# Local attention's output product moved behind its loop, an output copy put between exponentials, and the first image loaded by ACT's queue

## The chip, the cores and the metric

The kernel runs on one core of a Trainium2 chip. The metric is the device time of one execution in microseconds (us). Engines are called as in the profile: PE (TensorE, with its weight loads as PEld), DVE (VectorE), ACT (ScalarE), POOL (GpSimd), SP (SyncE, which here only issues DMAs; its queue is SPq).

## The reference

Two layers of a vision tower work on four images x of 64 channels x 128 steps x 64 variables. Cut to what matters:

```python
h = tok(x, W)                       # patches, rfft, projection: 1024 tokens x 64 for each image
h = h + local_attn(layernorm(h))    # the part that the change touches
h = h + moe_top2(layernorm(h))
h = h + full_attn_batchnorm(layernorm(h))
h = h + routed_moe(layernorm(h))
# local_attn: 16 query heads of 64, one key/value head, RoPE, RMS norm,
#   a token sees itself and the 128 before it; softmax; then
out = einsum('bqgts,bqgsd->bqgtd', attn, v).reshape(B, T, 16 * 64)
return out @ wo.T                   # 1024 tokens x 1024 -> 1024 x 64
```

## The kernel before, in words

The program is a row of stages, each a block with an instruction list for each engine and a barrier of all engines at its end that clears the semaphores. `setup` runs once; then `tokens`, `project`, `windowed`, `experts` and `full` run for each of the four images (a hardware loop); `batchnorm` and `routed` end it. The order inside a stage is written out by hand, engine by engine, with semaphore waits; no planner is involved.

**setup** (L286). SP issues 35 DMAs one after the other: two for the token weights (semaphore `tok_loaded`), 32 for all other constants, and last, through `load_x`, the 4 MB of image 0 into `xb`. It then waits until all but the first two have landed and raises `x_loaded`. DVE waits for that (L331) and then prepares the constants (`moe_w2`, the split bias, masks, `wqk`, `bvrep`), 5.7 us of work. Beside the loads PE makes 128 small products of the token weights (L360); after DVE's `h_ready` it makes two small ones (L364, L366), and after DVE has copied the token weights (`weff`) the first image's token products (L388: 8 pairs of matmuls with a 64-column weight and 512 moving columns, one to the upper and one to the lower 64 rows of a PSUM bank). ACT copies their result to `tokensT`.

**windowed** (L569). Local attention in 32 chunks of 32 tokens. A chunk passes through: scores on PE (L603 mask, L607 products) into banks 0-1 or 2-3; row maximum on DVE (L669) and the bias made of it (L672, `bias_ready`); four exponentials on ACT (L723, each with a sum); reciprocal on DVE (L688); scaling on POOL (L700, L702, `scaled`); transposes on PE (L627, L628, `turned` into banks 4-5); copy to `pT` on DVE (L682); value products on PE (L644, L641, `pv_done`) into banks 6-7; copy to `oT` (a view of `big2`) on ACT (L711, `oT_ready`). PE's list in step n is scores(n), turn(n-3), values(n-4). ACT's list in step n is the copy of chunk n-4, then the four exponentials of chunk n. scores(n) waits until the exponentials of chunk n-2 are done, since it writes their bank.

The output product with `wo` is made for each 128-token tile i in `out_product(i)` (L613): 8 matmuls with a 128-column piece of `oT` as the weight and 64 moving columns of `wo`. It stands inside `turn(c)` for c = 7, 11, ..., 31, ahead of that chunk's transposes, and DVE adds its result to `h` (L663) ahead of its `pT` copy. In steps 10, 14, ..., 30 six of them stand in the full loop; the seventh (c = 31) stands in the last steps, when scores are over; the eighth comes behind the loop. Then follow the layer norm on DVE, the transposes of `turn_normed` (L271) and the copies to `xT`.

**Other uses of the same helpers.** `turn_halves` (L392) makes four transposes of `tokensT` into bank 3; `tokens` calls it. SP loads the next image in `windowed`, at its start.

Of the kernel before, what the change touches and what calls it, by code (L numbers as in the profile page):

```python
# [25 lines left out]
P = 128  # L26
# [52 lines left out]
def program(nc, inp, out, sent_rows, answered_rows):  # L79
    with ExitStack() as ctx:  # L80
# [13 lines left out]
        big1 = sb("big1", [P, PAIRS, SEQ])  # L94
        big2 = sb("big2", [P, PAIRS, SEQ])
        aside = ("tok_w", "moe_w2")
        sbuf = {k: sb("s_" + k, *shapes[k]) for k in loaded if k not in aside}
# [94 lines left out]
        mean_row, var_row = sb("mean_row", [P, D]), sb("var_row", [P, D])  # L192
        first_sem = sem("const_loaded")
        sems = {n: sem(n) for n in [
# [6 lines left out]
        S = sems  # L201
        clear = range(first_sem.num, S["last"].num + 1)

        def stage(build):

            with nc.Block() as block:
                build(block)
            nc.all_engine_barrier(sems_to_clear=clear)  # L208

# [76 lines left out]
        def setup(block):  # L286
            @block.sync
            def _(sp):
                n = 0
                for k in ("tok_w", "dft"):  # L290
                    sp.dma_start(sbuf[k] if k in aside else sbuf[k][:], inp[k]).then_inc(S["tok_loaded"], 16)
                for k in loaded:
                    if k in ("tok_w", "dft"):
                        continue
                    sp.dma_start(sbuf[k] if k in aside else sbuf[k][:], inp[k]).then_inc(first_sem, 16)
                    n += 1
                for half in range(2):
                    r = slice(D * half, D * half + D)
                    for dst, src in ((row_of_t_rows, "row_of_t"), (window_mask_rows, "window_mask")):
                        sp.dma_start(dst[D * half:D * half + CHUNK], inp[src]).then_inc(first_sem, 16)  # L300
                        n += 1
                    for dst, src in ((qn, "q_norm"), (kn, "k_norm"), (bq, "bq1"), (bk, "bk1")):
                        sp.dma_start(dst[r, :], inp[src]).then_inc(first_sem, 16)
                        n += 1
                sp.dma_start(bvcol[:], inp["bv1"]).then_inc(first_sem, 16)
                n += 1
                for dst, src in ((blrow, "bl1"), (gammarow, "gamma"), (betarow, "beta"), (gate_b, "gate_b"),
                                 (moe_b2_rows, "moe_b2")):
                    sp.dma_start(dst[:] if dst is not moe_b2_rows else dst, inp[src].to_broadcast([P, inp[src].shape[1]])).then_inc(first_sem, 16)
                    n += 1  # L310
                load_x(sp, 0, first_sem)
                n += 1
                sp.wait_ge(first_sem, 16 * n)
                sp.sem_inc(S["x_loaded"], 1)

            @block.vector
            def _(v):
# [11 lines left out]
                ch.step(v.memset(moe_w2[:], 0.0))  # L329
                v.wait_ge(S["x_loaded"], 1)  # L330
                for r in range(2):  # L331
# [21 lines left out]
            @block.tensor  # L353
            def _(pe):
                pe.wait_ge(S["tok_loaded"], 32)
                w = sbuf["tok_w"]
                for o in range(D):
                    for j in range(2):

                        ins = nc.tensor.matmul(bank[0][D * j:D * j + D, o * STRIDE:(o + 1) * STRIDE], w[:, o, :],  # L360
                                               sbuf["dft"][:, j * STRIDE:(j + 1) * STRIDE], start=True, stop=True)
                ins.then_inc(S["tok_done"], 1)
                pe.wait_ge(S["h_ready"], 1)
                nc.tensor.matmul(bank[1][:, 0:D], bvrep[:], sbuf["wl1"][:], start=True, stop=True)  # L364
                for r in range(2):
                    ins = nc.tensor.matmul(bank[1][half_rows(r), D:2 * D], sbuf["wvT1"][:], sbuf["wl1"][:], start=True,  # L366
                                           stop=True)
                ins.then_inc(S["proj_done"], 1)
                pe.wait_ge(S["xn_ready"], 1)
                for r in range(STRIDE):  # L370
                    ins = token_products(r)
                ins.then_inc(S["prod_done"], 1)

            @block.scalar
            def _(a):
                a.wait_ge(S["prod_done"], 1)
                nc.scalar.activation(tokensT, bank[5][:], ACT.Copy)
# [48 lines left out]
        def project(block):  # L426
            @block.tensor
            def _(pe):
# [24 lines left out]
                def q_sums(hh):  # L453
# [6 lines left out]
                    for w in range(2):  # L460
# [4 lines left out]
                        ins.then_inc(S["ssq_done"], 1)  # L465

                for s in range(Q_SUMS[1] + 1):
                    if s < UNITS:
# [52 lines left out]
            def _(v):  # L521
                ch = Chain(v, S["dve_chain"])

                def q_sums(hh):

                    for w in range(2):
# [5 lines left out]
                                                None, ALU.add))  # L532

                for s in range(UNITS):
                    u, c = divmod(s, 2)
# [33 lines left out]
        def windowed(block, b):  # L569
# [11 lines left out]

            def added(c):
                return c % 4 == 3 and c >= 7

            def wo_at(i):
                return bank[5][:, HALF - D * (1 + i % 2):HALF - D * (i % 2)]

            @block.tensor
            def _(pe):
# [22 lines left out]

                def out_product(i):  # L613
                    pe.wait_ge(S["oT_ready"], NQ * (i + 1))
                    for p in range(PAIRS):
                        ins = nc.tensor.matmul(wo_at(i), oT[:, p, P * i:P * i + P], sbuf["wo0"][:, p, :], start=(p == 0),  # L616
                                               stop=(p == PAIRS - 1), skip_group_check=True)
                    return ins

                def turn(c):  # L620
                    pe.wait_ge(S["scaled"], c + 1)
                    if c >= 1:
                        pe.wait_ge(S["pT_ready"], c)
                    if added(c):
                        out_product((c - 7) // 4)
                    for q in range(NQ):
                        nc.tensor.transpose(bank[4][:, P * q:P * q + P], probs[:, c % 3, q, 0:P], ident[:])  # L627
                    nc.tensor.transpose(bank[5][:, 0:P], own[:, c % 2, :], ident[:]).then_inc(S["transposed"], 1)  # L628
# [19 lines left out]
                for n in range(CHUNKS + 4):  # L648
# [4 lines left out]
                    if n >= 4:  # L653
                        values(n - 4)
                out_product(TILES - 1).then_inc(S["wo_done"], 1)
                turn_normed(pe, 1)

            @block.vector
            def _(v):
                ch = Chain(v, S["dve_chain"])  # L660

                def add_out(i):
                    return v.tensor_tensor(h[:, i, :], h[:, i, :], wo_at(i), ALU.add)  # L663

                for n in range(CHUNKS + 3):
# [10 lines left out]
                    if c >= 0:  # L676
                        v.wait_ge(S["transposed"], c + 1)
                        if c >= 2:
                            v.wait_ge(S["pv_done"], c - 1)
                        if added(c):  # L680
                            add_out((c - 7) // 4)
                        v.tensor_copy(pT[:, c % 2, :],  # L682
# [6 lines left out]
                v.wait_ge(S["wo_done"], 1)  # L689
                ch.step(add_out(TILES - 1))  # L690
                layernorm(v, ch, h[:], xn_in_order, tmp, moe, st, TILES)
# [13 lines left out]
            @block.scalar  # L705
            def _(a):
                for n in range(CHUNKS + 4):
                    c = n - 4
                    if c >= 0:
                        a.wait_ge(S["pv_done"], c + 1)  # L710
                        nc.scalar.activation(  # L711
                            oT[:, :, CHUNK * c:CHUNK * (c + 1)].rearrange("p (h a) t -> p h a t", h=2),
                            ps[:, 6:8, 0:P].rearrange("p h (a t) -> p h a t", t=CHUNK),
                            ACT.Copy).then_inc(S["oT_ready"], 1)
                    c = n
                    if c < CHUNKS:
                        a.wait_ge(S["bias_ready"], c + 1)
                        if c >= 3:
                            a.wait_ge(S["transposed"], c - 2)
                        for e in range(2):  # L720
                            for hh in range(2):
                                q = 2 * e + hh
                                nc.scalar.activation(probs[:, c % 3, q, :],  # L723
                                                     bank[2 * (c % 2) + e][:, SPAN * hh:SPAN * hh + SPAN], ACT.Exp,
                                                     bias=small[:, c % 4, 1, q:q + 1], scale=rq[:, c, e, hh:hh + 1],
                                                     accum_out=small[:, c % 4, 2, q:q + 1]).then_inc(S["exp_done"], 1)
                turned_scalar(a, 1)
# [508 lines left out]
        with nc.Fori(0, IMAGES) as b:  # L1236
# [4 lines left out]
            stage(lambda block: full(block, b))  # L1241
        stage(batchnorm)
        stage(routed)
# [84 lines left out]
```

## Time and profile before

| | us |
|---|---|
| three timed runs | 1224.52, 1228.95, 1229.07 (median 1228.95) |
| the profiled execution's own time | 1223.5 |
| its span, first to last instruction | 1221.4 |
| setup, to the first image's copy by ACT | 0 to 51.6 |
| windowed of the first image, PE's first to last matmul | 109.0 to 216.5 |
| granted clock, mean | 0.839 |

The span is what the rows below are read from; about 2 us lie around it. Four windowed stages of some 107 us are a third of the time. A granted clock of 1.00 is 2.4 GHz, 0.50 is 1.2 GHz; a value between is a slice in which it changed. In the time before the first sustained work of PE the record shows 1.00 whatever the matmuls' durations are.

### The profile page before, as it was taken

Reading aid. Unit: us, or ns where it says so; the run is one execution under the profiler, and the core shown is the slowest. Engines: PE = TensorE matmul, PEld = TensorE weight load, DVE = VectorE, ACT = ScalarE, POOL = GpSimd, SP = SyncE. Lnnn points to the kernel's source line nnn. Section 1 sums busy time; section 2 is a strip of 40 time slices with the busy share of each in tenths; the row PEclk is TensorE's granted clock in tenths of the full one; section 3 lists DMA queues with packets and bytes.
Section 4 is the critical chain, followed back from the end, with each engine's and each line's share of the span. In section 5 each row is a group of like instructions: output and inputs, shape, how many; then the busy total and the mean of one; then the engine's idle time right before and its main releaser. Section 6 shows DMA issues by size and latency. Waiting matters only on the chain. (4 is left out here: it accounts for less than half of the span.)

```text
span 1221.4 us, 19579 instructions
## 1 busy us (share of the span) xinstructions
PE 848.1 (69%) x7278; PEld 579.6 (47%) x7278; DVE 689.3 (56%) x1470; ACT 441.1 (36%) x1363; POOL 338.9 (28%) x372
## 2 busy tenths in 40 slices
PE   4376997775869978858699787585997777120820
PEld 4133775554337755543377555433776455120620
DVE  0376665754766657537666574476665753830335
ACT  0023874232248742322487423224874232000200
POOL 0044543000445420004454200044543000027055
PEclk9987999897879998878799888778998889655865
DMA  7024000000330000003300000034000003000212
GB/s 239 35 54 151 2 2 2 1 1 3 62 143 2 2 2 1 1 3 61 144 2 2 2 1 1 2 56 149 2 2 2 1 1 97 8 8 26 72 40 45
DMA packets 51473, 43.52 MB, mean 36 GB/s; under 512 B 46484, under 2 KB 47956, under 8 KB 50452
## 3 DMA queue, kind: packets, MB, share of 16 engines
q1 hardware_dynamic: 49318, 40.03, 11.2%
q0 software_dynamic: 2048, 2.10, 0.6%
q8 instruction: 63, 1.03, 0.4%
q14 instruction: 44, 0.36, 0.1%
HBM read 29.33 MB, written 4.72 MB: 28 GB/s over the span
## 5 line engine op out<-in xcount | busy, mean ns | idle before, releaser
L723 ACT ACTIVATE work<-ps,small,rq 128x160 f32<-128x160 f32 x512 | 240.4, 487 | 50.7 <-DVE small L672 50.0
L700 POOL TENSOR_TENSOR work<-work,small 128x512 f32<-128x512 f32 x128 | 133.0, 1039 | 215.9 <-DVE small L688 215.9
L669 DVE TENSOR_REDUCE ps<-ps 128x4 f32<-128x640 f32 x128 | 106.5, 832 | 87.9 <-PE ps L607 87.9
L260 PE MATMUL ps<-xT,s_proj_w 64*128 64x512 f32 x384 | 120.6, 762 | 26.8 <-PEq L208 14.5
L682 DVE COPY pT<-ps 128x640 f32<-128x640 f32 x128 | 105.2, 822 | 5.0 <-PE ps L628 5.0
L723 ACT ACTIVATION_READ_ACCUMULATOR work<-ps,small,rq 128x1 f32 x512 | 106.9, 209 | 0.0
L607 PE MATMUL ps<-kT,big 64*128 64x160 f32 x1024 | 106.6, 331 | 0.0
L566 POOL TENSOR_TENSOR big<-xb 128x1024 f32<-128x1024 f32 x32 | 75.7, 2376 | 54.4 <-DVE xb L539 54.4
L260 PEld LDWEIGHTS ps<-xT,s_proj_w 64*128 64x128 f32 x384 | 45.5, 241 | 87.5 <-issue 63.9
L644 PE MATMUL ps<-pT,vwin 128*64 128x128 f32 x1024 | 84.2, 285 | 2.4 <-ACT big L711 2.4
L627 PE MATMUL ps<-s_ident,work 128*128 128x128 f32 x512 | 83.6, 286 | 1.4 <-DVE pT L682 1.2
L607 PEld LDWEIGHTS ps<-kT,big 64*128 64x128 f32 x1024 | 83.5, 207 | 0.4
L711 ACT ACTIVATE big<-ps 128x256 f32<-128x256 f32 x128 | 49.1, 384 | 89.7 <-PE ps L641 89.7
L616 PE MATMUL ps<-s_wo,big 128*128 128x64 f32 x512 | 65.7, 283 | 3.2 <-ACT big L711 2.0
L490 ACT ACTIVATE big<-ps 128x1024 f32<-128x1024 f32 x32 | 32.7, 1023 | 95.6 <-DVE xb L539 95.6
L627 PEld LDWEIGHTS ps<-s_ident,work 128*128 128x128 f32 x512 | 56.2, 146 | 19.8 <-issue 18.8
L616 PEld LDWEIGHTS ps<-s_wo,big 128*128 128x128 f32 x512 | 61.2, 196 | 9.2 <-issue 4.1
L559 POOL MEMSET vwin<- 128x256 f32 x4 | 1.2, 311 | 230.9 <-POOLq L208 230.9
L644 PEld LDWEIGHTS ps<-pT,vwin 128*64 128x64 f32 x1024 | 53.5, 136 | 24.1 <-issue 20.8
L1210 POOL DMA_INDIRECT sent_rows<-big,xb x32 | 30.9, 964 | 114.9 <-DVEq L1162 105.5
L884 PE MATMUL ps<-big 128*128 128x64 f32 x512 | 60.5, 273 | 0.0
L884 PEld LDWEIGHTS ps<-big 128*128 128x128 f32 x512 | 59.8, 193 | 0.0
(236 smaller groups left out, 1411.9 us busy)
## 6 DMA issues: line engine op xcount, KB each, us to landing
xb<-in_x SPq DMA_DIRECT2D x5, 4096.0 KB, 12.7
vrem<-xb SPq DMA_DIRECT2D x64, 64.0 KB, 2.1
s_proj_w<-in_proj_w SPq DMA_DIRECT2D x1, 1536.0 KB, 6.4
sent_rows<-zeros SPq DMA_DIRECT2D x8, 160.0 KB, 3.4
big<-sent_rows SPq DMA_DIRECT2D x5, 256.0 KB, 4.0
answered_rows<-big SPq DMA_DIRECT2D x8, 160.0 KB, 1.8
xb<-in_ffn_w SPq DMA_DIRECT2D x1, 1028.0 KB, 5.7
out<-vrem SPq DMA_DIRECT2D x8, 128.0 KB, 2.1
```

The source lines that it names most:

```text
L260: ins = nc.tensor.matmul(bank[banks + w][:], proj_w[half_rows(w), cols], xT[half_rows(w), :], start=True, stop=True)
L566: g.tensor_tensor(dst, first, second, ALU.add).then_inc(S["rot_done"], 1)
L607: ins = nc.tensor.matmul(tiles[e][:, hh, :], qT[half_rows(e), c, 4 * hh:4 * hh + 4, :].rearrange("p a t -> p (a t)"), kT[half_rows(e), CHU ...
L616: ins = nc.tensor.matmul(wo_at(i), oT[:, p, P * i:P * i + P], sbuf["wo0"][:, p, :], start=(p == 0), stop=(p == PAIRS - 1), skip_group_chec ...
L627: nc.tensor.transpose(bank[4][:, P * q:P * q + P], probs[:, c % 3, q, 0:P], ident[:])
L644: nc.tensor.matmul(o, vwin[:, c, :], pT[:, c % 2, P * q:P * q + P], start=True, stop=True, skip_group_check=True)
L669: ch.step(v.tensor_reduce(row_max(c), ps[:, s_banks(c), 0:2 * SPAN].rearrange("p e (h k) -> p e h k", h=2), X, ALU.max))
L682: v.tensor_copy(pT[:, c % 2, :], ps[:, 4:6, :].rearrange("p a n -> p (a n)")[:, 0:(NQ + 1) * P]).then_inc(S["pT_ready"], 1)
L700: g.tensor_tensor(probs[:, c % 3, :, 0:P], probs[:, c % 3, :, 0:P], bc(small[:, c % 4, 3, :], P), ALU.mult)
L711: nc.scalar.activation(oT[:, :, CHUNK * c:CHUNK * (c + 1)].rearrange("p (h a) t -> p h a t", h=2), ps[:, 6:8, 0:P].rearrange("p h (a t) -> ...
L723: nc.scalar.activation(probs[:, c % 3, q, :], bank[2 * (c % 2) + e][:, SPAN * hh:SPAN * hh + SPAN], ACT.Exp, bias=small[:, c % 4, 1, q:q + ...
L884: ins = nc.tensor.matmul(bank[6 + i % 2][:, 0:D], pT1[:, i % 2, P * k:P * k + P], v1[:, k, :], start=(k == 0), stop=(k == 7))
```

## The change

In `windowed`, `out_product` and its additions leave the loop. Behind it PE waits for all 32 chunks of `oT` and makes 16 products with `wo` as the 64-column weight and 512 tokens as moving columns; ACT copies the bank to `tokensT`, PE transposes it back (`turn_halves`), and DVE adds all 1024 tokens to `h` in one instruction. ACT's copy of chunk c-4 moves from ahead of the four exponentials of chunk c to between the second and the third. In `setup`, ACT issues the first image's load; SP issues first the constants that `setup` needs (`w_loaded`), then the others (`later_sem`, for which PE and DVE wait at the start of `project`), and only behind all of them waits for the first group and raises `set_ready`.

```diff
+        early = ("ident", "wvT1", "wl1", "moe_w2")
...
+        late = [k for k in loaded if k not in early and k not in ("tok_w", "dft")]
+        LATER = 16 * (len(late) + 5)
...
         def setup(block):
...
+                n = 0
+                for k in early:
+                    sp.dma_start(sbuf[k] if k in aside else sbuf[k][:], inp[k]).then_inc(S["w_loaded"], 16)
+                    n += 1
+                sp.dma_start(bvcol[:], inp["bv1"]).then_inc(S["w_loaded"], 16)
+                n += 1
+                for dst, src in ((moe_b2_rows, "moe_b2"), (blrow[:], "bl1")):
+                    sp.dma_start(dst, inp[src].to_broadcast([P, inp[src].shape[1]])).then_inc(S["w_loaded"], 16)
...
+                for k in late:
+                    sp.dma_start(sbuf[k][:], inp[k]).then_inc(later_sem, 16)
+                for half in range(2):
+                    sp.dma_start(bk[D * half:D * half + D, :], inp["bk1"]).then_inc(later_sem, 16)
+                for dst, src in ((gammarow, "gamma"), (betarow, "beta"), (gate_b, "gate_b")):
+                    sp.dma_start(dst[:], inp[src].to_broadcast([P, inp[src].shape[1]])).then_inc(later_sem, 16)
+                sp.wait_ge(S["w_loaded"], 16 * n)
+                sp.sem_inc(S["set_ready"], 1)
...
-                v.wait_ge(S["x_loaded"], 1)
+                v.wait_ge(S["set_ready"], 1)
...
                 pe.wait_ge(S["xn_ready"], 1)
+                pe.wait_ge(S["x_loaded"], 16)
...
+                load_x(nc.scalar, 0, S["x_loaded"])
                 a.wait_ge(S["prod_done"], 1)
...
+                pe.wait_ge(later_sem, LATER)
...
+                v.wait_ge(later_sem, LATER)
...
-                    if added(c):
-                        out_product((c - 7) // 4)
...
-                out_product(TILES - 1).then_inc(S["wo_done"], 1)
+                pe.wait_ge(S["oT_ready"], CHUNKS)
+                for p in range(PAIRS):
+                    for w in range(2):
+
+                        ins = nc.tensor.matmul(bank[0][D * w:D * w + D, :], sbuf["wo0"][:, p, :],
+                                               oT[:, p, w * HALF:(w + 1) * HALF], start=(p == 0), stop=(p == PAIRS - 1))
+                ins.then_inc(S["proj_done"], 1)
+                pe.wait_ge(S["v_act"], 1)
+                turn_halves(S["wo_done"])
                 turn_normed(pe, 1)
...
-                        if added(c):
-                            add_out((c - 7) // 4)
...
-                ch.step(add_out(TILES - 1))
+                by_half = h[:].rearrange("p (w j) d -> p j w d", w=2)
+                ch.step(v.tensor_tensor(by_half, by_half, bank[3][:].rearrange("p (j w d) -> p j w d", w=2, d=D),
+                                        ALU.add))
...
+                def outputs(c):
+                    a.wait_ge(S["pv_done"], c + 1)
+                    nc.scalar.activation(oT[:, :, CHUNK * c:CHUNK * (c + 1)].rearrange("p (h a) t -> p h a t", h=2),
+                                         ps[:, 6:8, 0:P].rearrange("p h (a t) -> p h a t", t=CHUNK),
+                                         ACT.Copy).then_inc(S["oT_ready"], 1)
+
+                for c in range(CHUNKS):
+                    a.wait_ge(S["bias_ready"], c + 1)
+                    if c >= 3:
+                        a.wait_ge(S["transposed"], c - 2)
+                    for q in range(NQ):
+                        if q == 2 and c >= 4:
+                            outputs(c - 4)
+                        e, hh = divmod(q, 2)
+                        nc.scalar.activation(probs[:, c % 3, q, :],
+                                             bank[2 * (c % 2) + e][:, SPAN * hh:SPAN * hh + SPAN], ACT.Exp,
+                                             bias=small[:, c % 4, 1, q:q + 1], scale=rq[:, c, e, hh:hh + 1],
+                                             accum_out=small[:, c % 4, 2, q:q + 1]).then_inc(S["exp_done"], 1)
+                for c in range(CHUNKS - 4, CHUNKS):
+                    outputs(c)
+                a.wait_ge(S["proj_done"], 1)
+                nc.scalar.activation(tokensT, bank[0][:], ACT.Copy).then_inc(S["v_act"], 1)
                 turned_scalar(a, 1)
```

## Rows read from the trace of the kernel before

**Rows 1.** The page: busy time of each engine (share of the span) and instructions.

```profile
PE 848.1 (69%) x7278; PEld 579.6 (47%) x7278; DVE 689.3 (56%) x1470; ACT 441.1 (36%) x1363; POOL 338.9 (28%) x372
```

**Rows 2.** Windows in the loop: bounds, length, busy by engine, clock, DMA share, GB/s.

```profile
128.00:133.00 5.00, 5.00 (x71) 3.55 (x66) 3.77 (x9) 4.52 (x19) 2.79 (x4) 1.00 0.00 0
```

**Rows 3.** Timeline, PE, image 1: start, duration, line, output<-input, count, idle before.

```profile
130.50 0.23 PE L603 MATMUL ps<-window_mask,row_of_t 64*128 64x128 bf16 x2
131.95 0.66 PE L644 MATMUL ps<-pT,vwin 128*64 128x128 f32 x8
132.54 0.45 PE L641 MATMUL ps<-pT,vrem 32*64 32x128 f32 x8
132.93 0.10 PEld L603 LDWEIGHTS ps<-window_mask,row_of_t 64*128 64x128 bf16 x2 [0.18 <-ACT work L723]
...
137.13 0.10 PEld L603 LDWEIGHTS ps<-window_mask,row_of_t 64*128 64x128 bf16 x2 [0.17 <-issue]
```

**Rows 4.** Timeline of ACT and DVE beside it.

```profile
130.63 0.38 ACT L711 ACTIVATE big<-ps 128x256 f32<-128x256 f32 x1 [0.19 <-PE ps L641]
130.91 0.48 ACT L723 ACTIVATE work<-ps,small,rq 128x160 f32<-128x160 f32 x1
132.24 0.16 DVE L672 SCALAR_TENSOR_TENSOR small<-ps,rq 128x4 f32<-128x4 f32 x1
132.66 0.21 ACT L723 ACTIVATION_READ_ACCUMULATOR work<-ps,small,rq 128x1 f32 x1
```

**Rows 5.** Timeline of the end of the loop and of the tail, image 1.

```profile
201.22 2.00 PE L616 MATMUL ps<-s_wo,big 128*128 128x64 f32 x16 [0.29 <-POOL pTr_own L702]
203.05 0.61 PE L627 MATMUL ps<-s_ident,work 128*128 128x128 f32 x4
...
206.43 0.38 ACT L711 ACTIVATE big<-ps 128x256 f32<-128x256 f32 x1 [1.25 <-PE ps L641]
206.87 2.00 PE L616 MATMUL ps<-s_wo,big 128*128 128x64 f32 x16 [0.50 <-ACT big L711]
208.90 0.22 DVE L663 TENSOR_TENSOR h<-h,ps 128x64 f32<-128x64 f32 x1 [4.14 <-PE ps L616]
```

**Rows 6.** Timeline: token products in `experts` and `setup`, their copy, an addition, transposes.

```profile
238.47 7.09 PE L388 MATMUL ps<-xb,weff 128*64 128x512 f32 x32
245.60 0.60 ACT L787 ACTIVATE work<-ps 128x512 f32<-128x512 f32 x1 [18.98 <-PE ps L388]
239.88 0.68 DVE L816 TENSOR_TENSOR turned<-ps,comb 128x512 f32<-128x512 f32 x1
...
42.04 8.92 PE L388 MATMUL ps<-xb,weff 128*64 128x512 f32 x32
52.78 0.63 PE L395 MATMUL ps<-s_ident,work 128*128 128x128 f32 x4 [1.82 <-PEq L208]
```

**Rows 7.** Timeline of the tail's product, image 3.

```profile
693.34 2.82 PE L616 MATMUL ps<-s_wo,big 128*128 128x64 f32 x16 [0.50 <-ACT big L711]
```

**Rows 8.** Windows of that tail: columns as in Rows 2.

```profile
694.00:695.00 1.00, 1.00 (x9) 1.00 (x7) 0.00 (x0) 0.00 (x0) 0.00 (x0) 0.65 0.00 0
```

**Rows 9.** Timeline of `setup`: SP's first and last issue, PE, DVE.

```profile
0.75 0.43 SPq L291 DMA_DIRECT2D big<-in_tok_w  x1
5.62 13.83 PE L360 MATMUL ps<-s_dft,big 18*64 18x8 f32 x256 [5.62 <-DMA s_dft<-in_dft]
20.39 0.43 SPq L381 DMA_DIRECT2D xb<-in_x  x1
35.19 0.59 DVE L333 COPY moe_w<-big 64x256 f32<-64x256 f32 x2 [30.76 <-SPq L314]
41.02 0.68 PE L364 MATMUL ps<-s_wl,bvrep 64*128 64x64 f32 x2 [21.57 <-DVEq L346]
```

**Rows 10.** Windows of `setup`, DVE alone: bounds, length, busy, clock, DMA share, GB/s.

```profile
0.00:20.00 20.00, 3.04 (x12) 1.00 0.65 193
20.00:33.00 13.00, 0.00 (x0) 1.00 0.98 345
```

More of the change, by code:

```diff
@@ L192, in program @@
         mean_row, var_row = sb("mean_row", [P, D]), sb("var_row", [P, D])
-        first_sem = sem("const_loaded")
+        later_sem = sem("later_loaded")
         sems = {n: sem(n) for n in [
@@ L201, in program, with stage @@
         S = sems
-        clear = range(first_sem.num, S["last"].num + 1)
-        def stage(build):
+        late = [k for k in loaded if k not in early and k not in ("tok_w", "dft")]
+        LATER = 16 * (len(late) + 5)
+        def stage(build, first=later_sem.num + 1):
             with nc.Block() as block:
                 build(block)
-            nc.all_engine_barrier(sems_to_clear=clear)
+            nc.all_engine_barrier(sems_to_clear=range(first, S["last"].num + 1))
         def bc(ap, n):
@@ L288, in _ @@
             def _(sp):
-                n = 0
                 for k in ("tok_w", "dft"):
                     sp.dma_start(sbuf[k] if k in aside else sbuf[k][:], inp[k]).then_inc(S["tok_loaded"], 16)
[L292 to L295, printed above, removed]
+                n = 0
[6 more added lines that the diff above has]
+                    sp.dma_start(dst, inp[src].to_broadcast([P, inp[src].shape[1]])).then_inc(S["w_loaded"], 16)
                     n += 1
@@ L299, in _ @@
                     for dst, src in ((row_of_t_rows, "row_of_t"), (window_mask_rows, "window_mask")):
-                        sp.dma_start(dst[D * half:D * half + CHUNK], inp[src]).then_inc(first_sem, 16)
+                        sp.dma_start(dst[D * half:D * half + CHUNK], inp[src]).then_inc(S["w_loaded"], 16)
                         n += 1
-                    for dst, src in ((qn, "q_norm"), (kn, "k_norm"), (bq, "bq1"), (bk, "bk1")):
-                        sp.dma_start(dst[r, :], inp[src]).then_inc(first_sem, 16)
+                    for dst, src in ((qn, "q_norm"), (kn, "k_norm"), (bq, "bq1")):
+                        sp.dma_start(dst[r, :], inp[src]).then_inc(S["w_loaded"], 16)
                         n += 1
[L305 to L314, printed above, removed]
+                for k in late:
[6 more added lines that the diff above has]
+                sp.sem_inc(S["set_ready"], 1)
             @block.vector
@@ L580, in row_max @@
                 return ps[:, s_banks(c), HALF - 2:HALF]
[L582 to L586, printed above, removed]
             @block.tensor
@@ L611, in scores @@
                     ins.then_inc(S["scores_done"], 1)
[L613 to L618, printed above, removed]
                 def turn(c):
@@ L660, in _ @@
                 ch = Chain(v, S["dve_chain"])
-                def add_out(i):
-                    return v.tensor_tensor(h[:, i, :], h[:, i, :], wo_at(i), ALU.add)
                 for n in range(CHUNKS + 3):
@@ L706, in _ @@
             def _(a):
[L707 to L726, printed above, removed]
@@ L1241, in program @@
             stage(lambda block: full(block, b))
-        stage(batchnorm)
+        stage(batchnorm, later_sem.num)
         stage(routed)
```

## The prediction

> **What bounds the kernel now.** I read the page first: PE is busiest, but with 69% of the span [rows 1], so no engine bounds the whole and each stage has to be read by itself. Then the windows of the loop of local attention: there PE is busy in all of 5.00 us at clock 1.00, ACT in 4.52, DVE in 3.77, POOL in 2.79 [rows 2]. Then the timeline of one step. Scores start at 130.50 and again at 132.93, 2.43 us a step. At 132.93 PE has stood 0.18 us and the releaser is ACT's last exponential, so it looks as if ACT set the pace. But at 137.13, behind a step with the output product, the same gap is 0.17 with nothing waited for [rows 3]: it is what PE shows at any wait, and the wait for ACT adds 0.01. PE and ACT are level, and PE's own work is some 2.42 a step. So what leaves PE's list in the loop shortens it, and what moves on ACT alone gains nearly nothing.
>
> In `setup` I read the timeline. SP issues from 0.75 on, one DMA per 0.4 to 1.0 us, and gets to the image, the last of 35, at 20.39; DVE starts on the constants at 35.19, PE's next product comes at 41.02, and PE has stood since 19.45 [rows 9]. The chain is SP's issuing, the image's landing (14.8 us), DVE's 5.8 us.
>
> **Loop: six products leave (windowed, each image).** The step with a product takes 132.93 to 137.13, 4.20, the others 2.43 [rows 3]: 1.77 each, six of them 10.6 us. The addition on DVE goes with it. Bounds: at most 2.00, the product's own span [rows 5]; at least 1.77 less what the next bound leaves. That is ACT: four exponentials and the copy fill 130.63 to 132.87, 2.24 us [rows 4], below 2.42, so it covers nothing.
>
> **The seventh and the wait on POOL.** In the last steps the product stands at 201.22 and the transposes behind it start at 203.05 [rows 5]: 1.83 us come back, since what they wait for was there at 201.22.
>
> **ACT's copy between the exponentials.** Before, the exponentials of a step stood behind the copy: 130.91 though the bias is ready at 132.24 + 0.16 = 132.40 for the scores of 130.50, and those exponentials come at 133.3, 0.9 later [rows 4]. Now two start at the bias, 1.9 us into the step, and the copy follows 0.92 later, at 2.8; the value products that it waits for end at 132.54 + 0.45, 2.49 into the step [rows 3]. It does not wait. The next value products need that copy at 131.95 - 130.50 = 1.45 into the next step, 3.87; the copy ends at 3.2. The last exponentials end some 4.2 into the step, and PE needs them at 4.84. So all three slacks (0.3, 0.6, 0.6 us) are open, and the gain is the 0.01 a step, 0.3 us a stage. In the last steps POOL's data come earlier, for which PE stood 0.29 [rows 5]: 0.3 more. Zero at the least; at the most 0.9, by which the exponentials move.
>
> **The new tail.** Before, from the last copy's end at 206.81 to the end of the addition at 208.90 + 0.22: 2.3 us [rows 5]. Now 16 products of 64 weight columns and 512 moving ones. The token products have this very shape, number and column halves: 238.47 to ACT's start at 245.60, 7.13 us at full clock [rows 6]. Then ACT's copy 0.60, four transposes 0.63, an addition of 512 columns out of PSUM 0.68 [rows 6], and four hand-overs of 0.06 (206.87 less 206.81). Sum 9.3, so 7.0 more than before. All of it lies on the path, since the layer norm needs it. One stage: 10.6 + 1.8 + 0.6 - 7.0 = 6.0 us gained, four 24.0.
>
> **Clock in the tail.** In image 3 the tail's product took 2.82 instead of 2.00 [rows 5, 7], and the window of 694 to 695 shows 0.65, between the two levels [rows 8]: PE had stood in short waits before, and the clock fell to 1.2 GHz while the product ran. The long product comes behind the same thin steps, thinner by one product. The token products of `setup`, which ran half their time at half speed, took 8.92 [rows 6], 1.8 over 7.13. Bounds: nothing, or the whole at half, 7.1 more. I take 1.8 in three images of four, 5.4, less the 0.8 that images 3 and 4 pay already, 1.6: 3.8 us lost. Windowed: 24.0 - 3.8 = 20.2 gained.
>
> The Trainium skill has a rule on this ("TensorE: Matmul & The Clock Gate", Part 1: The HAM clock gate): slow is the default, and activity releases it, so dense work soon runs at full speed. By it a dense product cannot stay slow to its end; the trace agrees so far as the products of `setup`, 8.92 where all slow would be 14.3 [rows 6]. The sum goes by the rows without it.
>
> **Setup.** ACT has nothing else to do, so the image is issued by about 2 us and, with its 14.8 from issue to use [rows 9], is there at 17. SP issues 34 instead of 35, all before it waits: `set_ready` cannot come before 20.4, although the last DMA that it needs is the 19th and long landed. That is the next thing late: DVE starts at 20.5 instead of 35.19, 14.7 earlier. Behind it all keeps its distance: PE's small products at 26.3, the token products 42.04 - 14.7 = 27.3. PE's first work (5.62 to 19.45) has 6.8 us of cover if its weights land later beside the image. The late constants are issued by 20.4; even with the image's 14.8 they are there at 35.2, and `setup` does not end before 51.6 - 14.7 = 36.9. The waits for them in `project` cost nothing.
>
> What speaks against it is that both queues share the DMA engines. In 0 to 20 they were 0.65 busy, in 20 to 33 0.98 [rows 10]: 25.7 us of full work in all, so if everything went ahead of the image it would land at 27, at the moment when it is needed. Gain 14.7; lower bound 11 (SP's issues slowed, or its small loads 3 us late), upper 16.5 (the products no longer start at half speed, 1.8).
>
> The skill says the same of the engines ("DMA: Bandwidth & Descriptors", Issuing engines are not separate DMA queues): issuing on several only saves the sequencer's time, "which is usually small relative to the DMA itself". By that sentence the move would save some 0.43 us. The trace speaks otherwise here, since the time saved is 34 issues ahead of the image, 19.6 us [rows 9], more than its transfer.
>
> **Sum.** 20.2 + 14.7 = 34.9 us. The profiled execution took 1223.5, the median of the runs shown is 1228.95, the lowest 1224.52; one leads to 1188.6, the other to 1194.0. I take 1191.
>
> **Rivals.**
> (a) The tail's product stays at half speed to its end in all images: 7.1 each instead of 5.4 in all. 28.4 - 5.4 = 23 us back, 1214. For it: the clock does fall there. Against: it rose again within the products of `setup`.
> (b) The shared DMA engines: the image or SP's small loads come so late that `setup` gains 4 instead of 14.7: 1202. For: 345 GB/s at 0.98 busy when the image ran [rows 10]. Against: the sum of 25.7.
> (c) Slower: with the products gone PE's clock falls inside the loop. PE's step at half clock grows by at most 2.42; with 1.7 (between that and nothing, nearer to it since PE is busy throughout), it decides from 35 / 1.7 = 21 of 128 steps on. If it held for one image's 28 full steps: 48 us lost, 1191 + 48 = 1239. Against: PE is 5.00 of 5.00 busy in steps without a product at clock 1.00 [rows 2].
> (d) The change does not do what it says: ACT and PE hold each other, so a step without the product stays level with the worst of the mixed ones, or the copy comes too late for the value products. Each 0.1 us a step costs 11 us: at 0.2, 1213. Against: the three slacks.
>
> **Numbers.** Forecast 0.76 (own range 1184 to 1198), (a) 0.07, (b) 0.08, (c) 0.04, (d) 0.05. The range of 1181 to 1204 holds forecast and (b). No change that a measurement can tell is within 0.5%, 6 us, of 1229. Faster: forecast, (a) and (b), most of (d): 0.93. Slower: (c), 0.04. Same 0.03.
>
> **What would show it.** Right: steps of 2.42 all through the loop; the first exponential 1.9 us behind the scores; a tail product of 7.1 to 9 us; DVE's first copy in `setup` at 20.5 and the token products at 27.3. Wrong: scores waiting for ACT by more than 0.2; a tail product near 14; `setup`'s token products released by the image's DMA; a granted clock of 0.50 within the loop.

## The result, and the profile after

| | before | changed |
|---|---|---|
| median of 4 runs, us | 1228.51 (1224.52 to 1229.07) | 1193.66 (1192.98 to 1194.29) |
| profiled execution, us | 1223.5 | 1194.13 |
| its span, us | 1221.4 | 1192.3 |

Ratio 0.9723, 95% interval 0.9701 to 0.9745: 34.9 us less, where 34.9 were worked out and 1191 was forecast. Between the two profiled executions it is only 29: that of before lies at the lower edge of the 13 runs of the kernel before in a later comparison (1223.22 to 1230.19, median 1228.43). The sum came out right; two of its terms did not, and they had opposite signs. Every stage time below is read from one execution of each kernel, and of the kernel before that is one of the faster ones.

The loop, to be held against [rows 2 to 4]: a window of the changed kernel (its columns are those of rows 2), then its timeline of PE, DVE and ACT.

```profile
150.00:155.00 5.00, 5.00 (x68) 3.60 (x64) 3.64 (x8) 4.65 (x21) 2.95 (x5) 1.00 0.00 0
```

```profile
151.28 0.16 DVE L669 SCALAR_TENSOR_TENSOR small<-ps,rq 128x4 f32<-128x4 f32 x1
151.48 0.48 ACT L718 ACTIVATE work<-ps,small,rq 128x160 f32<-128x160 f32 x1 [0.17 <-DVE small L669]
...
151.96 0.23 PE L604 MATMUL ps<-window_mask,row_of_t 64*128 64x128 bf16 x2
152.42 0.38 ACT L706 ACTIVATE big<-ps 128x256 f32<-128x256 f32 x1
...
154.38 0.10 PEld L604 LDWEIGHTS ps<-window_mask,row_of_t 64*128 64x128 bf16 x2 [0.17 <-issue]
```

Steps are 2.42 us (151.96 to 154.38). The first exponential of the scores of 151.96 comes at 153.91, 1.95 behind them. The copy (152.42) stands between the second and the third exponential, and the scores wait for nothing. ACT now stands 0.17 ahead of its first exponential and is busy in 4.65 of 5.00 us, PE in all 5.00: ACT has slack, PE has none.

The tail of image 1 [rows 5]: timeline of the changed kernel.

```profile
185.88 0.38 ACT L706 ACTIVATE big<-ps 128x256 f32<-128x256 f32 x1 [1.25 <-PE ps L633]
186.31 7.09 PE L651 MATMUL ps<-big,s_wo 128*64 128x512 f32 x32 [0.50 <-ACT big L706]
193.45 0.60 ACT L725 ACTIVATE work<-ps 128x512 f32<-128x512 f32 x1 [7.19 <-PE ps L651]
194.10 0.66 PE L400 MATMUL ps<-s_ident,work 128*128 128x128 f32 x4 [0.70 <-ACT work L725]
```

`setup` [rows 9]: timeline of the changed kernel (SP's slowest and its last issue among them), then a row of its DMA view for 0 to 40 us (size, median us from issue to landing). The DMA view of the kernel before gave 4.2 for `s_ident`. For `qn`, two loads of 0.2 KB, the two views have 4.6 before and 8.1 changed.

```profile
0.75 0.39 ACTq L386 DMA_DIRECT2D xb<-in_x  x1
7.89 2.91 SPq L308 DMA_DIRECT2D bq<-in_bq  x1
11.57 13.82 PE L363 MATMUL ps<-s_dft,big 18*64 18x8 f32 x256 [11.57 <-DMA s_dft<-in_dft]
24.82 0.45 SPq L315 DMA_DIRECT2D gate_b<-in_gate_b  x1
25.43 0.59 DVE L336 COPY moe_w<-big 64x256 f32<-64x256 f32 x2 [21.01 <-SPq L317]
32.29 9.92 PE L393 MATMUL ps<-xb,weff 128*64 128x512 f32 x32
```

```profile
s_ident<-in_ident SPq DMA_DIRECT2D x1, 64.0 KB, 13.1
```

Where the time went, by stage, read off the timelines. `S` is from the start to ACT's copy of the first image to `h`. The other columns have the images 1 to 4: `project`, `windowed` and `experts` run from PE's first product to that of the next stage, `full` to ACT's copy of the next image to `h` (for image 4 to the first product of `batchnorm`), and `rest` from there to DVE's last instruction. Between ACT's copy to `h` and `project` lie 10.0 us for each image, 9.5 to 10.0 in all rows, which stand in no column. The same for the experiments on local attention and the clock; after_again is the changed kernel a second time.

```
                 S      project                   windowed                      experts                   full                      rest
before         53.44  45.62 46.73 46.08 46.42  109.00 109.00 110.45 110.13  33.11 32.96 33.51 33.45  43.83 45.22 45.86 41.06  192.55
changed        44.68  46.83 47.07 47.32 47.40  102.90 102.89 102.89 102.98  34.19 32.75 32.85 32.82  44.61 45.83 45.80 41.20  194.42
after_again    44.20  45.66 46.60 47.41 46.64  103.00 103.14 102.90 103.19  34.18 32.93 32.89 32.97  44.50 45.85 46.09 41.20  194.13
setup_alone    43.41  46.58 46.12 46.24 46.12  110.38 110.43 110.39 110.43
product_alone  54.26  45.09 47.33 46.58 46.59  103.65 103.41 103.51 103.57
order_alone    53.55  46.41 47.25 46.27 46.91  109.10 108.48 109.09 108.49
old_shape_b.   44.68  45.89 45.93 47.33 47.32  108.97 108.97 108.97 108.96
phase_shift    47.14  46.85 47.46 46.42 46.41  103.00 102.93 103.55 103.26                           44.31 45.19 46.31 41.07  192.45
tail_idle      44.57  46.75 46.93 46.92 46.68  106.71 106.80 106.82 106.71
```

`setup` gave 8.8 us, the four windowed stages 6.1, 6.1, 7.6 and 7.2, in all 26.9; in this pair of executions the stages that the change does not touch took 6.7 back, 3.8 of it in `project`. Windows of PE in `project` of image 3 (bounds, length, busy, granted clock), before and then changed, show why: the clock is 0.83 and 0.75, and the same work takes 46.1 and 47.3 us.

```profile
548.80:594.88 46.08, 31.22 (x141) 0.83 0.25 44
```

```profile
531.62:578.94 47.32, 33.26 (x140) 0.75 0.24 43
```

This holds in all 16 windows of `project` of before, changed, after_again and phase_shift: 45.6 to 45.7 us where the clock is 0.84, 46.1 to 46.4 at 0.83, 46.6 to 47.1 at 0.79, 47.3 to 47.5 at 0.75. The changed kernel alone, run twice, moves between them: 46.83 and 45.66 in image 1.

### The profile page after: what moved, and what is told of

It is laid out like the page before. It is cut to its first block and busy times, and to the rows that moved or that the text cites. A ratio compares the mean times of both kernels' runs of the same rounds, so it can differ in the third digit from the quotient of the medians.

```text
span 1192.3 us, 18816 instructions
## 1 busy us (share of the span) xinstructions
PE 826.7 (69%) x6902; PEld 533.4 (45%) x6910; DVE 685.6 (58%) x1442; ACT 443.6 (37%) x1367; POOL 338.5 (28%) x372
## 5 line engine op out<-in xcount | busy, mean ns | idle before, releaser
L718 ACT ACTIVATE work<-ps,small,rq 128x160 f32<-128x160 f32 x512 | 243.5, 485 | 71.5 <-DVE small L669 71.0
L262 PE MATMUL ps<-xT,s_proj_w 64*128 64x512 f32 x384 | 123.4, 778 | 26.7 <-PEq L210 14.6
L677 DVE COPY pT<-ps 128x640 f32<-128x640 f32 x128 | 105.4, 824 | 10.4 <-PE ps L620 10.4
L718 ACT ACTIVATION_READ_ACCUMULATOR work<-ps,small,rq 128x1 f32 x512 | 104.4, 204 | 0.0
L273 PE MATMUL ps<-s_ident,vwin 128*128 128x128 f32 x48 | 12.0, 397 | 68.3 <-DVE vwin L229 68.3
L633 PE MATMUL ps<-pT,vrem 32*64 32x128 f32 x1024 | 57.3, 293 | 0.0
L604 PE MATMUL ps<-window_mask,row_of_t 64*128 64x128 bf16 (+1 forms) x256 | 33.1, 254 | 33.5 <-PEq L210 23.6
```

The lines of the kernel that those rows point to most:

```text
L262: ins = nc.tensor.matmul(bank[banks + w][:], proj_w[half_rows(w), cols], xT[half_rows(w), :], start=True, stop=True)
L633: ins = nc.tensor.matmul(o, vrem[r, c, :], pT[r, c % 2, NQ * P:], start=False, stop=True, tile_position=(CHUNK * q, D * e), skip_group_che ...
L677: v.tensor_copy(pT[:, c % 2, :], ps[:, 4:6, :].rearrange("p a n -> p (a n)")[:, 0:(NQ + 1) * P]).then_inc(S["pT_ready"], 1)
L718: nc.scalar.activation(probs[:, c % 3, q, :], bank[2 * (c % 2) + e][:, SPAN * hh:SPAN * hh + SPAN], ACT.Exp, bias=small[:, c % 4, 1, q:q + ...
```

## The experiments

Medians and ratios are against the kernel before, run beside each on the same chip. Its median was 1228.43 for setup_alone, product_alone, order_alone and old_shape_behind, 1228.72 for after_again, dve_waits_itself, image_after_tok and both_setup, and 1227.37 for the other four.

### One part at a time: setup_alone, product_alone, order_alone

```diff
# setup_alone: the changed kernel with
-        def windowed(block, b): ...   (changed)
+        def windowed(block, b): ...   (before)
# product_alone: the kernel before, with PE's and DVE's lists of windowed changed; ACT keeps its order and gets
+                a.wait_ge(S["proj_done"], 1)
+                nc.scalar.activation(tokensT, bank[0][:], ACT.Copy).then_inc(S["v_act"], 1)
# order_alone: the kernel before, with outputs(c - 4) between the second and third exponential
```

> The setup edit alone, local attention as before. Theory: DVE's first copy of the constants comes at 25.4 us and the token products at 32.3, as in the changed kernel (35.19 and 42.04 before), so setup gives 8.8 us by ACT's copy of the first image; the four windowed stages stay at 109 to 110.5 us each; other stages move by a few us either way with the clock. Time 6 to 12 us under the kernel before. Rival: the late constants cost the first project stage what setup gains, and it takes over 50 us where it took 45.6; then the time moves by less than 4.

> The output product behind the loop, ACT's copies ahead of the exponentials as before, setup as before. Theory (PE sets the pace of the loop): steps without a product are 2.43 us as before, the stage loses 10.6 us of products, 1.8 in the last steps, and gains a tail of 6.9 to 7.0, so a windowed stage takes 103.5 us instead of 109.0, and the whole is 22 us under the kernel before. Rival (ACT sets the pace and only the new order frees PE): steps grow over 2.45 once the products no longer give ACT its slack, and a stage takes over 105.

> Only ACT's copy between the exponentials; products in the loop, setup as before. Theory: steps without a product 2.42 instead of 2.43, with one 4.20, the last steps 0.3 shorter: 0.6 us a stage, 2.4 in all, hardly to be told from nothing. Rival: the order is what made the loop faster, and a stage takes 107 or less; or it costs, with value products waiting for the later copy, and a stage takes over 109.5.

| | median, us | ratio (95%) |
|---|---|---|
| setup_alone | 1218.04 | 0.9910 (0.9892 to 0.9928) |
| product_alone | 1199.62 | 0.9767 (0.9746 to 0.9788) |
| order_alone | 1223.46 | 0.9955 (0.9939 to 0.9972) |

The stage times came as expected for the setup alone (110.4, where 109 to 110.5 was expected) and for the product alone (103.4 to 103.7, where 103.5 was); the order alone took 108.5 in two images and 109.1 in the other two, where 108.4 was expected in all. The whole gained more than expected in two of the three: 28.8 instead of 22 by the product, 5.0 instead of 2.4 by the order. The rival in which ACT sets the pace falls with this timeline of product_alone, where the old order stands without the products:

```profile
150.38 0.10 PEld L597 LDWEIGHTS ps<-window_mask,row_of_t 64*128 64x128 bf16 x2 [0.18 <-ACT work L713]
...
152.81 0.10 PEld L597 LDWEIGHTS ps<-window_mask,row_of_t 64*128 64x128 bf16 x2 [0.18 <-ACT work L713]
```

2.43 with 0.18 of standing, as before; 0.01 a step is all that the order is worth there. The three gains, 10.4, 28.8 and 5.0 by medians, add up to 44, the whole gave 34.9. Between profiled executions the same three are 3.5, 20.3 and 0.5, 24 in all, and the whole 29. In `windowed` itself they nearly add up: 24.4 by the product and 3.4 by the order, and 26.9 by both. What does not add up lies in the other stages and between executions of one kernel, which spread over 7 us for the kernel before. That parts which shift the rest in time shift also where the clock falls is the likely reason; no run shows it as the whole of it.

setup_alone has `windowed` unchanged, and all four of its stages take 110.4 where before has two at 109.0. The tail's old product, in its timeline, makes 0.8 of that: 2.73 to 2.81 us where the clock falls in it, 2.00 where not [rows 5, 7].

```profile
444.30 2.81 PE L623 MATMUL ps<-s_wo,big 128*128 128x64 f32 x16 [0.50 <-ACT big L718]
```

The other 0.6 lies ahead of the last output copy, at the stage's start. The stage starts at clock 0.50. In image 1 of before it is back at 1.00 by 118.0, 9 us in, in image 3 it is still 0.50 at 603.9 to 604.9, and the last copy comes 97.4 and 98.0 us into the stage. order_alone keeps the old product, and in its four images it took 2.00 each, behind the same 0.50 of standing. Its images of 109.1 are those with the late rise at the start. So more than half of what the order gained in images 3 and 4 is that the tail kept its clock: 1.7 of 3.0 us.

### Place or shape: old_shape_behind

```diff
# on PE; left out here: turn_halves, ACT's copy and DVE's regrouping go as well
-                for p in range(PAIRS):
-                    for w in range(2):
-                        ins = nc.tensor.matmul(bank[0][D * w:D * w + D, :], sbuf["wo0"][:, p, :],
-                                               oT[:, p, w * HALF:(w + 1) * HALF], start=(p == 0), stop=(p == PAIRS - 1))
...
+                for i in range(TILES):
+                    for p in range(PAIRS):
+                        ins = nc.tensor.matmul(bank[3][:, D * i:D * i + D], oT[:, p, P * i:P * i + P],
+                                               sbuf["wo0"][:, p, :], start=(p == 0), stop=(p == PAIRS - 1),
+                                               skip_group_check=True)
+                ins.then_inc(S["wo_done"], 1)
...
```

> The changed kernel, but behind the loop the product has its old shape: 64 products with 128 columns of oT as the weight and 64 moving columns of wo, all eight tiles into one bank, added to h in one instruction; no copy by ACT and no transposes back. Theory (the shape gives the gain, the place none, since PE is the bound in the loop and alone in the tail): eight times 1.86 us, 14.9, in place of 7.13 + 0.60 + 0.63 + two hand-overs, 8.5: a windowed stage of 109.3 instead of 102.9 and the whole 25 us over the changed kernel. Rival (leaving the loop is the gain, since the product delayed DVE, ACT and POOL there too): a stage under 105.

Measured: 1219.09, ratio 0.9925 (0.9906 to 0.9944), 25 us over the changed kernel, and stages of 108.97 (109.3 expected), level with the kernel before. Its timeline of the tail:

```profile
185.38 14.51 PE L650 MATMUL ps<-s_wo,big 128*128 128x64 f32 x128 [0.50 <-ACT big L702]
```

14.51 against 7.09. Leaving the loop gave nothing; the shape gave it, 6.1 us a stage after its copy and transposes are paid. The shape is two things at once: the small matrix as the weight with 512 moving columns, and two products beside each other, one to the upper and one to the lower 64 rows of the bank. No run has one without the other, so what each gives is not shown.

### The clock: tail_idle and phase_shift

```diff
# tail_idle, on ACT behind the last output copy; PE waits for oT_ready CHUNKS + 1
+                for spare in (work[:, 0:HALF], work[:, HALF:2 * HALF], work[:, 3 * HALF:], turned[:, 0:HALF],
+                              turned[:, HALF:]):
+                    ins = nc.scalar.activation(spare, bank[4][:], ACT.Copy)
+                ins.then_inc(S["oT_ready"], 1)
# phase_shift, on DVE in setup ahead of the constants
+                for _ in range(10):
+                    ch.step(v.memset(moe_w2[:, 0, :], 0.0))
```

> The changed kernel with five dummy copies on ACT (0.6 us each) behind the last output copy of local attention, for which PE waits: PE stands 3 us more ahead of the tail's product. If the clock in the tail hangs on the thin steps ahead of it, it now falls there, and the product takes 8.9 to 10.7 us in most images instead of 7.1: stages of 107.5 to 109.5 and the whole 18 to 26 us longer. If not, the stage grows by the 3 us alone, to 105.9, and the whole by 12.

> The changed kernel with ten memsets of some 0.1 us more, each behind the other, on DVE in setup, ahead of the constants: a pure delay of 1 to 2 us. Theory (in the stages that the change does not touch, the time hangs on where the clock's falls and rises come): their times move by up to 1.5 us each, project between 45 and 47.5, full between 43.8 and 46.2, and the whole moves by other than the delay, between -3 and +6. Rival (it does not): every stage takes what it took, and the whole is longer by the delay alone.

tail_idle: 1204.91 (0.9824, 0.9799 to 0.9849), 11 us over the changed kernel, with stages of 106.7 to 106.8. Timeline, then windows of PE (length, busy, granted clock) in image 1:

```profile
188.56 8.45 PE L651 MATMUL ps<-big,s_wo 128*64 128x512 f32 x32 [2.95 <-ACT turned L726]
```

```profile
188.00:189.00 1.00, 0.43 (x2) 0.50 0.00 0
...
191.00:192.00 1.00, 1.00 (x6) 0.82 0.00 0
```

With 2.95 us of standing the clock falls while PE stands (0.97 in 187 to 188), is at 1.2 GHz when the product starts, and back at 2.4 during 191 to 192. It costs 1.4 us (8.45 to 8.56 against 7.09), less than the 1.8 expected at the least: a stage grew by 3.85, 2.45 of delay and 1.4 of clock, between the two outcomes that were set down (105.9, and 107.5 to 109.5). Behind the thin steps of the changed kernel (the last ones, in which scores are over and PE's waits are 0.3 to 0.6 us), with 0.50 of standing, the product ran at full clock in all four images, and in all four again in a repeat (after_again).

> The changed kernel again, beside the three setup variants on the same chip: 1193 to 1194 us, windowed stages of 102.9 each, DVE's first copy at 25.4.

1193.88 (0.9727, 0.9708 to 0.9746), stages of 102.9 to 103.2.

phase_shift: 1193.23 (0.9732, 0.9706 to 0.9758). `S` is 2.5 us longer (47.14), and the median is that of the changed kernel, 1193.66 and 1193.88. In the profiled execution the delay was made up in stages that nobody touched (`rest` 192.45 instead of 194.42, `project` of images 3 and 4 about 1 less). But this run cannot tell a delay that costs nothing from one that costs its 2.5 us: with it the ratio would be 0.9743 or 0.9747, inside the interval, and `project` moves by up to 1.2 us between two executions of the changed kernel without any delay. That the stage times hang on where the clock's falls and rises come is borne out by the clocks of the 16 windows above; that a delay of the start moves them is not shown. Against it stands setup_alone, whose `S` is 10.0 us shorter and whose median is 10.4 lower: there the whole of `setup`'s gain came through, by the medians.

### What holds setup: four variants

```diff
# dve_waits_itself
-                sp.wait_ge(S["w_loaded"], 16 * n)
-                sp.sem_inc(S["set_ready"], 1)
-                v.wait_ge(S["set_ready"], 1)
+                v.wait_ge(S["w_loaded"], 16 * 17)
# image_after_tok, on ACT
+                a.wait_ge(S["tok_loaded"], 32)
                 load_x(nc.scalar, 0, S["x_loaded"])
# both_setup: the two together
# tokens_first_image_later: both, and on DVE the copy of weff, on PE the token products, ahead of the constants
# tokens_first_late_last: that, and on SP
+                sp.wait_ge(S["x_loaded"], 16)
                 for k in late:
```

> The changed kernel, but DVE waits for the first group of loads itself instead of for SP, which raises its flag only behind the issue of all late loads. Theory: SP's issuing held DVE back (25.43); the last load that DVE needs is issued by 16.4 and lands some 3 us later, so DVE starts at 19.5 and is done at 25.3, PE's token weight products end at 25.4 anyway, and the first image's token products start at 26.6 instead of 32.3: 5.7 us less in setup. Rival: the loads themselves are late beside the image, they land at about 25, and nothing is gained.

> The changed kernel, but ACT issues the image only when the token weights and the DFT matrix have landed. Theory (the image's transfer delayed them from 5.6 to 11.57 and slowed SP's issues, 2.91 us for one of them): PE's first products start at 5.6 again and end at 19.4; SP's slow issues move behind the image's issue or go, so DVE starts between 20.5 and 25.4; the image is there by about 21. Gain 0 to 5 us. Rival (SP's issues are slow by themselves once the order is another): DVE starts at 25.4 as before, no gain.

> Both edits together. Theory: PE's first products run from 5.6 to 19.4, DVE's constants are ready by 25 or earlier, the image by 21, and the token products start at 24 to 26.6 instead of 32.3: 6 to 8 us less than the changed kernel, 1186 to 1188 us. Rival: the image becomes the last thing (over 27), and the pair gives less than the wait alone.

> The changed kernel with three edits in setup: DVE copies weff before it waits for the constants, PE makes the token products ahead of its two small ones, and ACT issues the image only when the token weights are in; DVE waits for its loads itself. Theory (the image shares the DMA engines with every other load): PE's first products 5.6 to 19.4, the token products as soon as the image has landed. In the trace of the run with both edits the engines are full from 12 to 30 us, and the last load that DVE needs, issued at 10.99, landed at 25.5; if the image lands as late, the token products start at about 25 and setup ends 9 us before that of the changed kernel's 42.9: 1185. If the image lands at 20.5 (14.8 behind its issue, as alone), they start at 20.5: 1181.

> As tokens_first_image_later, and SP issues the late constants only when the image is in. Theory (the late loads, 2.7 MB, take half of the engines from the image): the image lands by 18 to 20, the token products start at 19.5 to 20.5, and setup ends 14 us before the changed kernel's, unless DVE's constants then end it: they land by 15 to 20 and take 6 us. The late constants land by 33 and the first project stage, at about 40, does not wait. 1180 us. Rival: the late loads delay the project stage, which then takes over 50 us.

| | DVE's constants start | token products start | S ends | median, us | ratio (95%) |
|---|---|---|---|---|---|
| changed | 25.43 | 32.29 | 44.68 | 1193.66 | 0.9723 (0.9701 to 0.9745) |
| dve_waits_itself | 20.05 | 26.90 | 38.22 | 1189.88 | 0.9673 (0.9657 to 0.9690) |
| image_after_tok | 27.49 | 34.35 | 46.20 | 1196.31 | 0.9729 (0.9714 to 0.9744) |
| both_setup | 25.60 | 32.46 | 44.58 | 1192.76 | 0.9703 (0.9687 to 0.9718) |
| tokens_first_image_later | 25.20 | 23.68 | 36.95 | 1188.33 | 0.9689 (0.9663 to 0.9715) |
| tokens_first_late_last | 24.93 | 23.66 | 35.18 | 1186.55 | 0.9678 (0.9654 to 0.9703) |

dve_waits_itself came as expected: SP's list, not the loads, released DVE in the changed kernel; the last load needed landed at 20.05, as its timeline shows. It is 6.5 us less in `S` and 4 in the whole.

```profile
20.05 0.59 DVE L334 COPY moe_w<-big 64x256 f32<-64x256 f32 x2 [15.63 <-DMA bq<-in_bq]
```

image_after_tok and both_setup missed (a gain of 0 to 5 and of 6 to 8 us was expected; the medians are 2.7 over and 0.9 under the changed kernel's). The timeline of both_setup shows what I had not reckoned with.

```profile
10.99 0.60 SPq L308 DMA_DIRECT2D bq<-in_bq  x1
...
13.69 5.39 SPq L311 DMA_DIRECT2D s_by_head<-in_by_head  x1
...
25.60 0.59 DVE L334 COPY moe_w<-big 64x256 f32<-64x256 f32 x2 [21.18 <-DMA bq<-in_bq]
```

A load of 0.2 KB issued at 10.99, behind the image's issue at 5.57, landed at 25.6, 1.7 behind the image (18.3 from issue to landing), and SP's issuing stood: one issue took 5.39 us, in image_after_tok 5.68. The last two variants put the token products ahead of the constants, so that only the image is waited for (PE's row: 4.32 us, by the DMA). Holding the late constants back did not make it land earlier (23.66 against 23.68), so my expectation that they take half of the engines from it fell: 18.0 us from issue to landing in both, by the DMA view. The two came out at 1188.33 and 1186.55, where 1185 (or 1181) and 1180 were expected. The last variant is the fastest kernel here, 7 us under the changed one by the medians (from two comparisons; the intervals just overlap, 0.9654 to 0.9703 and 0.9701 to 0.9745).

## Why the prediction was right

- **Six products at 1.77 and the seventh at 1.83, the order 0.6**: 13.0 was worked out from the stage's start to the last copy; measured 97.4 (206.43 less 109.04) and 84.4 (185.88 less 101.48), 13.0. The total is confirmed, and product_alone confirms that PE bounds the loop with ACT level behind it. Both stages start with the clock back at 1.00 after some 9 us, so this pair is free of the 0.6 that a late rise costs.
- **The tail, 7.0 more**: from the last copy to the next stage 11.6 before and 18.5 changed, 6.9. The token products as a model of the new product were exact (7.09 both).
- **The clock in the tail, 3.8 lost**: wrong. It was not lost in any image. What failed is the step from the old tail's 2.82 to the new one: the old product fell to half in images 3 and 4 of before and in all four of setup_alone, the long one in none of the changed kernel, of after_again or of product_alone; with 2.95 us of standing ahead of it it took 8.45 (tail_idle). The old product itself, with the same 0.50 of standing, kept its clock in all four images of order_alone. So neither the shape nor that wait alone makes the clock fall, and why it fell in some stages and not in others stays open. Instead 2.6 us came back that the images 3 and 4 had paid (stages of 110.45 and 110.13 against 109.00): 1.7 in the tail's product (2.82 and 2.87 against 2.00) and 0.9 ahead of it.
- **Setup, 14.7**: too much; 8.8 measured in `S`. The failed step is `set_ready` at 20.4: SP's issues were taken at their old pace, 19.6 us for 34, but beside the image they take 24.5 and reach 25.3. That is 4.9 of the 5.9 us. The other 1.0 is in the token products, 9.92 instead of 8.92, for which the sum had nothing or a gain of 1.8. The bound of 11 "by SP's issues slowed, or its small loads 3 us late" named the right mechanism with too small a size. The loads were late as well, `s_ident` in 13.1 us instead of 4.2, but that did not set the time: dve_waits_itself has all that DVE needs at 20.05. PE's first products, which wait for `s_dft`, started at 11.57 instead of 5.62 and used up 6.0 of their 6.8 us of cover. Rival (b) had late loads, with a gain of 4; the measured gain lies midway.
- **Nothing elsewhere**: wrong by 6.7 us in the profiled pair; no term stood for the stages that are not touched. By the medians it is about 1 (26.9 and 8.8 against 34.9), if these two are what they are in the pair. The difference is that the profiled execution of before is 5 us under its median; in which stages a run of 1228.5 spends these 5 us no trace shows.
- **1223.5 or 1228.95**: I took a point between. The comparison went by the median, and 1228.51 less the worked out 34.9 would have been 1193.6.

The errors of the clock and of `setup` (26.9 against 20.2, and 8.8 against 14.7) cancel almost exactly, and that is luck. So is that the stages which the sum left out show up in the profiled pair and hardly in the medians. The right sum is no proof of its terms; the stage table is what checks each.

## What to carry to other kernels

Here a product whose weight changes each 64 moving columns cost PE twice what the same product cost with the small matrix as the weight, 512 columns moving and two products beside each other (14.51 and 7.09); where PE is the bound, count that and not the place. Before a large load is moved beside small ones, ask which small ones are waited for, since they landed late beside it, and who waits behind the issues of the queue, since those slowed down too. Read a saving per stage, since a stage that is not touched gave or took up to 2 us here with the clock, and take more than one execution before a few us are explained.

## What the runs showed of the hardware

- Loads of 0.2 to 64 KB issued on SP's queue while ACT's queue moved 4 MB took 7 to 13 us instead of 3 to 5 (changed kernel), or 14 where they were issued behind it (`qn`, `bq` in both_setup); the DMA view has the image as 144 packets on its queue (29 KB each) and the rest as thousands of small ones. One issue on SP took up to 5.7 us in that time (image_after_tok), and no more than 1.0 in the kernel before.
- The clock of PE fell within 2.95 us of standing and was back at 2.4 GHz at 192, with PE busy from 188.56 on (tail_idle). Behind waits of 0.3 to 0.6 us it did not fall in the long product (changed kernel, after_again, product_alone: 7.09 in all twelve images); in the old product it fell in two images of four (before), in four (setup_alone) and in none (order_alone), behind the same waits but for one of 0.3 us.
- The `project` stage took 45.6 us where its granted clock was 0.84 and 47.5 where it was 0.75; two executions of one kernel had 46.83 at 0.79 and 45.66 at 0.84 for the same image (changed, after_again).
- With a delay of 2.5 us in `setup` the whole took 1193.23, and 1193.66 and 1193.88 without (phase_shift); the intervals, 3 us wide to each side, do not exclude that it costs its length.
